# Four of six transposes of h moved from TensorE to VectorE and DMA, in a fused attention and FP4 feed-forward kernel

## The reference, cut to what matters

```python
Q = _xpos(X @ W_Q); K = _xpos(X @ W_K, downscale=True); V = X @ W_V     # X: 8 x 1024 x 256
p = softmax(Q @ K.T) * 0.9 ** abs(n - m)
x = _layernorm(X + p @ V)
h = silu(fp4_linear(x, w_gate)) * fp4_linear(x, w_up)                    # 256 -> 704
out = _layernorm(x + fp4_linear(h, w_down))                              # 704 -> 256
# fp4_linear rounds x and w to FP4 in blocks of 16 (a scale for each block), then multiplies
```

## Time and profile before

| | |
|---|---|
| median of 3 runs | 980.66 us (979.34 to 980.86) |
| time of the profiled execution | 980.01 us |
| its span, first to last instruction | 978.1 us |
| PE busy | 960.3 us (98%) |
| DVE busy | 866.3 us (89%) |
| POOL busy | 786.9 us (80%) |
| ACT busy | 641.3 us (66%) |

### The profile page before, as it was taken

How to read it: one execution, slowest core, us unless ns; L and a number is a source line. 1 busy time by engine, 2 the same in 40 slices (tenths; PEclk the granted TensorE clock), 3 DMA queues, 4 the chain that set the end, 5 groups by cost and what they waited for, 6 DMA issues and landing times.

```text
span 978.1 us, 20226 instructions
## 1 busy us (share of the span) xinstructions
PE 960.3 (98%) x6002; PEld 869.6 (89%) x6002; DVE 866.3 (89%) x1995; ACT 641.3 (66%) x1576; POOL 786.9 (80%) x854
## 2 busy tenths in 40 slices
PE   8999999999999999999999999999999999999996
PEld 7788998989998999998998899888999899899886
DVE  6979988988988988999898898888898898999985
ACT  3656666677666667666667666657666667777664
POOL 5988888798888889788788888879787888877664
PEclk9999999999999999999999999999999999999999
DMA  9124244342433424324343434433243342333300
GB/s 319 45 84 132 93 136 125 103 136 82 154 106 97 144 84 152 122 82 133 110 141 113 136 98 139 121 105 126 93 146 104 108 136 82 98 108 109 104 22 22
DMA packets 116109, 111.25 MB, mean 114 GB/s; under 512 B 12576, under 2 KB 93728, under 8 KB 114080
## 3 DMA queue, kind: packets, MB, share of 16 engines
q1 hardware_dynamic: 115312, 108.91, 34.7%
q10 hardware_dynamic: 688, 1.05, 0.3%
HBM read 69.53 MB, written 40.37 MB: 112 GB/s over the span
## 4 chain that ended last, share of the span: by engine, by line
PE 88%; DVE 6%; issue 2%; DMA 2%; POOL 1%; SPq 1%; ACT 0%; POOLq 0%; DVEq 0%; ACTq 0%
PE ps_g L634 12%; PE ps_g L635 11%; PE ps_g L636 11%; PE ps_oy L634 9%; PE ps_oy L636 9%; PE ps_oy L635 9%; PE ps_s L634 6%; PE ps_s L635 6%; PE ps_s L636 6%; PE ps_t L643 4%; PE ps_oy L643 1%; DMA parking<-turned 1%; PE ps_oy L822 1%; PE ps_oy L821 1%; PE ps_s L683 1%
## 5 line engine op out<-in xcount | busy, mean ns | idle before, releaser
L2478 POOL TENSOR_TENSOR h<-h,hsc 128x704 f32<-128x704 f32 x126 | 168.5, 1337 | 77.1 <-DVE h L1843 43.2
L2585 POOL TENSOR_TENSOR prob<-prob,decay_t 128x512 f32<-128x512 f32 x128 | 164.0, 1298 | 0.5 <-ACT prob L1282 0.5
L634 PE MATMUL ps_g<-wgu_h,xqt_h 128*128 128x480 f32 (+1 forms) x380 | 148.8, 392 | 2.8 <-DVE xqt_l L1898 1.2
L634 PE MATMUL ps_oy<-v_h,pt_h 128*128 128x256 f32 x512 | 149.0, 291 | 0.1
L635 PE MATMUL ps_oy<-v_l,pt_h 128*128 128x256 f32 x512 | 144.7, 283 | 0.0
L636 PE MATMUL ps_oy<-v_h,pt_l 128*128 128x256 f32 x512 | 144.7, 283 | 0.0
L636 PE MATMUL ps_g<-wgu_h,xqt_l 128*128 128x480 f32 (+1 forms) x380 | 142.6, 375 | 0.0
L635 PE MATMUL ps_g<-wgu_l,xqt_h 128*128 128x480 f32 (+1 forms) x380 | 142.3, 374 | 0.0
L1794 DVE SCALAR_TENSOR_TENSOR th<-th,ps_g 128x240 f32<-128x240 f32 x183 | 72.0, 397 | 49.4 <-ACT th L1212 47.9
L634 PE MATMUL ps_s<-k_h,q_h 128*128 128x512 f32 x256 | 102.8, 402 | 0.0
L635 PE MATMUL ps_s<-k_l,q_h 128*128 128x512 f32 x256 | 100.1, 391 | 0.0
(11 more groups left out here) (273 smaller groups left out, 3106.3 us busy)
## 6 DMA issues: line engine op xcount, KB each, us to landing
parking<-turned SPq DMA_DIRECT2D x122, 256.0 KB, 2.0
landing<-parking SPq DMA_DIRECT2D x488, 64.0 KB, 2.0
rope_t<-rope SPq DMA_DIRECT2D x15, 1024.0 KB, 5.9
xres<-x SPq DMA_DIRECT2D x64, 128.0 KB, 2.1
out<-yout SPq DMA_DIRECT2D x63, 128.0 KB, 2.0
xin<-x_t SPq DMA_DIRECT2D x14, 512.0 KB, 4.3
first_rope<-rope SPq DMA_DIRECT2D x2, 512.0 KB, 7.5
decay_t<-decay SPq DMA_DIRECT2D x1, 960.0 KB, 12.1
```

Source lines behind the costliest of these rows:

```text
L634: pe.matmul(dst, a_h, b_h, start=(start and i == 0), stop=False)
L2478: return tt(blocks(dst), blocks(src), sc[:, which, at:at + n].unsqueeze(2).to_broadcast([P, n, QB]), ALU.mult)
L2585: tt(prob[:, keys], prob[:, keys], decay_t[:, lo:lo + CW], ALU.mult).then_inc(decayed, 1)
```

## The change: what it does

1. For tiles 0 to 58 (`turns(i)`), squares 0 to 3 of h no longer go through TensorE. VectorE turns them (`turn_h`, 128 x 512 from `h` to `turned[:, 0]`, the buffer that half 0 of the probabilities uses too), SyncE parks them in a new HBM buffer `h_parking` and lands them by four DMAs in a new buffer `h_landing`. ScalarE makes `ht_h` from it (`h_landed_high`) and also copies it to `ps_t[:, 0]` (`h_landed_copied`), and VectorE makes `ht_l` from there as before. `h_transposes(i, 1)`, two squares, stays on TensorE and comes in the next step. Tiles 59 to 63 stay as they were.
2. The copy of half 1 of the landed probabilities to PSUM and VectorE's subtraction are gone. GpSimd subtracts both halves (`landed_low(i, g)`).
3. `down` comes a step later (`down(six)`), and with it `second_residual`, `r2_mean`, `r2_squares`; `output` and `store` go to `seven`; `R2_BEHIND` is 4.
4. The buffer `th` is gone (its room is `h_landing`); the activation of the gate is written to `h` itself.
5. The order of the calls is new in every step of every engine.

```diff
-R2_BEHIND = 3
+R2_BEHIND = 4
+LAST_TURNED = LAST_TILE - 5
...
+def turns(i):
+
+    return 0 <= i <= LAST_TURNED
+
+
+def h_turns(i, g):
+
+    return 2 * i + (g + 1 if i > LAST_TURNED else 2 - g)
+
+
+def h_transposed(i, g):
+
+    return i + 1 if i <= LAST_TURNED else 2 * i + g - LAST_TURNED
...
+            def park_h(i):
+                if turns(i):
+
+                    sp.wait_ge(h_turned, i + 1)
+                    wait(sp, h_landed, 16 * QUADS * (i - 1))
+                    sp.dma_start(h_parking[i % 2], turned[:, 0, :]).then_inc(h_parked, 16)
+
+            def land_h(i):
+                if turns(i):
+
+                    sp.wait_ge(h_parked, 16 * (i + 1))
+                    wait(sp, htl_done, 2 * i)
+                    if i == 0:
+                        sp.wait_ge(wqkvl_done, 3)
+                    rows = h_parking[i % 2].rearrange("(a j) (c x) -> c j a x", a=QUADS, c=QUADS)
+                    for c in (0, 2, 1, 3):
+                        sp.dma_start(h_landing[c * QUAD:(c + 1) * QUAD, :].rearrange("p (a x) -> p a x", a=QUADS),
+                                     rows[c]).then_inc(h_landed, 16)
...
                 elif j == 6:
-                    scores(now, 0)
-                    down(five)
+                    h_transposes(five, 1)
+                    down(six)
                     projection()
...
                     gate_up(three, 1)
-                    h_transposes(four, 0)
-                    h_transposes(four, 1)
                     gate_up(three, 2)
...
+            def h_landed_high(i):
+                if turns(i):
+
+                    act.wait_ge(h_landed, 16 * QUADS * (i + 1))
+                    wait(act, y_done, i)
+                    nc.scalar.copy(keys_by_quad(ht_h[:, 0:4, :]), h_landed_at).then_inc(hth_done, 1)
+
+            def h_landed_copied(i):
+                if turns(i):
+
+                    act.wait_ge(h_landed, 16 * QUADS * (i + 1))
+                    nc.scalar.copy(keys_by_quad(ps_t[:, 0]), h_landed_at).then_inc(h_copied, 1)
...
-            def landed_copied(i):
-                if crosses(i):
-
-                    act.wait_ge(landed[1], 16 * QUADS * crossing(i))
-                    wait(act, ptl_done[1], i)
-                    wait(act, htl_done, 2 * (i - 3) + 2)
-                    nc.scalar.copy(keys_by_quad(ps_t[:, 1]), landed_half(1)).then_inc(copied, 1)
...
+            def turn_h(i):
+                if turns(i):
+
+                    dve.wait_ge(hq_done, 2 * i + 1)
+                    if crosses(i + 3):
+                        dve.wait_ge(parked[0], 16 * crossing(i + 3))
+                    nc.vector.transpose(turned[:, 0, :].rearrange("p (c n q) -> p n c q", c=QUADS, n=4),
+                                        h[:, i % 2, 0:CW]).then_inc(h_turned, 1)
...
+                    if g == 0 and turns(i - 4):
+                        dve.wait_ge(h_parked, 16 * (i - 3))
...
-            def landed_low(i):
-                if crosses(i):
-
-                    dve.wait_ge(copied, crossing(i))
-                    dve.wait_ge(pth_done[1], i + 1)
-                    wait(dve, o_done, i)
-                    keys = half_of_keys(1)
-                    tt(pt_l[:, keys, :], ps_t[:, 1], pt_h[:, keys, :].bitcast(F32), ALU.subtract)\
-                        .then_inc(ptl_done[1], 1)
...
+            def landed_low(i, g):
                 if crosses(i):
+                    pool.wait_ge(pth_done[g], i + 1)
+                    wait(pool, (o_first_done, o_done)[g], i)
+                    keys = half_of_keys(g)
+                    tt(keys_by_quad(pt_l[:, keys, :]), landed_half(g), keys_by_quad(pt_h[:, keys, :]).bitcast(F32),
+                       ALU.subtract).then_inc(ptl_done[g], 1)
```

More of the change, by code:

```diff
@@ L925, in step @@
             def step(s):
-                now, one, two, three, four, five, six = (s - lag for lag in range(7))
+                now, one, two, three, four, five, six, seven = (s - lag for lag in range(8))
                 j = s % NT
```

1076 lines of the change are left out of this document (557 added, 519 removed).

## The result

| | before | after |
|---|---|---|
| median of 4 runs | 980.04 us (979.34 to 980.86) | 1024.91 us (1023.34 to 1027.14) |
| ratio | 1 | 1.0461 (1.0444 to 1.0477) |
| span of the profiled execution | 978.1 us | 1021.5 us |

The account below looks back on a forecast made before the run. TensorE, busy for 98% of the span, was taken as the bound. From 980.7 us, 25.4 saved (59 tiles x 0.43) and 5.5 lost to late landings gave 960.8, say 961 us; range 954 to 977 us.

Parts of the forecast that it names:

- I cost it at nothing: ScalarE's wait for h's landing: at most 2 us late, covered by other work; without cover up to 2 us a step.
- in a like manner: Step j = 1: the 1 MB table stands ahead of h as the load of x does ahead of half 1 in j = 2.
- 0.8 us a batch for both: TensorE's loss from late landings in j = 1 and 2: between 0 and 1.9 us a batch, 5.5 us over 7 batches.
- the 4 that I estimated: The turn of h on VectorE is done some 4 us before the step ends, TensorE still having two parts of gate and up.
- So what leaves TensorE comes off the batch: TensorE alone sets the period: 0.43 us a tile saved, 25.4 us for 59 tiles, until another engine runs out of room.
- The queue holds it on average: SyncE's five added DMAs take 4.1 us a step, against 5.0 us it stands idle waiting for `turned`.
- its price: GpSimd's `pt_l` of half 1: 1300 ns, 10.4 us a batch, making 107.35 of 113.3 us, 95%.
- rivals B and C: GpSimd's idle waits leave it short of room: B (0.20), 966 to 978.7 us; C (0.17), slower than before.
- C: GpSimd becomes slower than TensorE was, above 1.2 us idle a step; at 1.5 us, 1000 us; chance 0.17.
- `turn(one, 0)` would wait for the park of h: VectorE's turn into `turned[:, 0]` found waiting until h has left it; named as a sign that the forecast is wrong.
- The high-load latency: HBM answering in 2 us at high load: each hop of h and the probabilities 1.8 us later; no sign of it seen.
- the loss-free 955 of the forecast: The kernel's time with TensorE's 25.4 us saved and nothing lost to late landings: 955 us.

Follow-up runs that it names:

- rope_short: The changed kernel with the load of the table of cosines cut to 4 of its 128 partitions: 991.92 us, 1.0106.
- rope_behind_h: The changed kernel with the 1 MB table issued behind the landing of h in steps j = 1: 1007.49 us, 1.0271.
- the last kernel: The changed kernel with the table load cut, h's five DMAs left out, GpSimd's second `pt_l` on a quarter and `row_max` on half its columns: 985.29 us, 1.005.
- before_four_squares_out: The kernel before with squares 0 to 3 of h not transposed for tiles 0 to 58 and nothing in their place: 973.81 us, 0.9922.

## Why the prediction was wrong, point by point

- **"I cost it at nothing"** (h's crossing) is the step that failed by most. I wrote that the table in j = 1 stands ahead of h "in a like manner" to the load of x in j = 2, and took 0.8 us a batch for both; the table alone cost 5.4 (122.5 less 117.1 in `rope_short`). The park took 6.0 us behind 1 MB, where my sum had 2.0; ScalarE, waiting for it with `x1_high` behind, passed the delay to TensorE: 33 us (`rope_short`), about half of them back by moving the table alone (`rope_behind_h`). The turn of h ended at 507.42, 2.0 us ahead of the last matmul of gate and up (509.45), not the 4 that I estimated. Some 8 of the 33 us are the clock of 1.2 GHz behind the holes, for which the prediction has no term. The row that would have told was in the trace: a landing 4.3 us behind 512 KB.
- **"So what leaves TensorE comes off the batch"** is the second step that failed. The size of what leaves, 0.66 - 0.23 = 0.43 us a tile, was right (0.43 in the steps j = 3). But in the others the squares stood in a place where TensorE would else have waited for its bank, in the step of the earlier trace rows until 0.14 us before it went on. Measured, 7.5 us for 25.4 in the old order; in the new order, where the two squares that stay have left that place as well, nothing of it is seen: the step j = 6 takes 15.1 us in `rope_short` and 15.1 before. The Trainium skill (Perfetto Trace Analysis, Matmuls) advises that matmul groups rotate through different banks, so that emptying one overlaps the next group. The rows agree, and show its edge: three parts on two banks leave 1.50 us, from the start of part 0's last matmul to the end of part 1, for the 0.41 + 0.41 + 0.43 + 0.40 + 0.16 = 1.81 us of emptying, and the squares filled the rest.
- **ScalarE's and SyncE's room as averages.** "The queue holds it on average" is true, and it says nothing of single steps: behind a table, or in the short steps at the end, where the chain that ended last ran through the queue, the copies and VectorE.
- **The last batch** was not looked at by itself: 6.9 us lost, where 2.6 were to be gained. Most of that is the order, not the crossing: without the DMAs of h the six steps still take 81.2 us of 82.3.
- **GpSimd**: its price was right (1296 ns, 106.6 us a batch for 107.35 forecast), and the mechanism of rivals B and C is not what came: cut to a quarter, the new `pt_l` gives 0.6, 1.0 and 1.7 us. C had the sign, with 0.17, and named "late landings of h" as another road to it; its example was 1000 us. That `turn(one, 0)` would wait for the park of h hardly happened: 0.2 us, once.
- **DMA latency.** The medians stayed at 2.0 to 2.1 us at 144 to 147 GB/s. The high-load latency of the Trainium skill (DMA: Bandwidth & Descriptors, Latency and other measured facts) is not seen at this load; what made the park late was the table issued ahead of it (`rope_short`, `rope_behind_h`). The same page (Queues, rings and completion order) says that an engine works off the descriptors of one ring in order; the 5.98 us agree. Whether it is that order or the DMA engines shared with 1 MB, no run tells apart: the table from another engine's queue was not tried.

The sum: 980.0 + 33.0 (table) + 4.1 (crossing) + 1.7 (`pt_l`) + 0.8 (`row_max`) + 4.8 (rest of the new order) = 1024.4 of 1024.9 us; the order in which the causes were removed may shift a us or two between them, and the 1.7 and 0.8 are within the spread of the executions. Against the loss-free 955 of the forecast the 985.3 us of the last kernel are 30 us too much: 3.1 us a batch for 6.3 batches, 19 us, and 8 us in the last six steps (80.9 for 72.8). The 4.8 us of the rest lie in those last steps too (80.9 us for 75.4 before); the batch, 116.4 us, is then that of before (116.6), although TensorE has four squares less in each step. Left open is which single chain holds the batch at 115.4 to 115.9 us once four squares are out of the old order: each one that was shortened gave 1 to 2 us. What part 2 of the change costs in the old order is open too. No version of the changed kernel beat the one before; the only gains seen, 7 to 9 us, are from work left out without anything in its place, and so belong to no kernel that computes the result.

## What to carry to other kernels

An engine that is busy for 98% is not proof that what leaves it comes off the time: look at what the next instruction on it waits for, and when that was ready. Here the answer was 0.14 us earlier in the step read, 0.1 to 0.3 in most, and of 0.43 us a tile 0.13 came off. Before a short transfer on a critical path is added to a queue, find the largest transfer that can stand ahead of it, and count its full duration, in that step, against the cover of that step; averages over a batch hide both. A long hole on TensorE can cost more than its length: look at the granted clock behind it. And when an edit takes away the reason of a wait, take the wait away too, or the experiment measures that.

## What the runs showed of the hardware that was not expected

- A park of 256 KB issued 0.86 us behind a load of 1 MB on the same queue was seen as done 5.98 us later (the queue waited up to 6.7 us for one in the changed kernel), against 2.1 us in the median; behind the same load cut to a thirty-second it took 2.16 us.
- In `after`, behind each of six holes of 2.4 to 3.4 us on TensorE, the granted clock was 0.50 (1.2 GHz in place of 2.4) while TensorE worked again; gate and up took 5.3 us there, in place of 4.0.
- Six transposes of 128 x 128 cost 0.66 us of TensorE's time, two 0.23: four are 0.43 us (1.09 less 0.66, steps j = 3 of `before` and `before_four_squares_out`).
- From the start of the last matmul of a part to ScalarE reading it 0.41 us, ScalarE to VectorE 0.41, the two operations of VectorE 0.43 and 0.40, and 0.16 us from there to TensorE (`after`, step j = 2 shown above).
